# A graph layer on one core: two residual pieces go to GpSimd, tile 14's moments to ScalarE, and tile 14's result to the very end

## The reference

```python
h = jnp.maximum(_layernorm(x, axis=-1), 0.0)
x = x + _L0_gnn_ref(h, adj, ...)      # adj @ round(relu(q(h) @ q(weight))), 4-bit activations, 3-bit weights
h = jnp.maximum(_layernorm(x, axis=-1), 0.0)
x = x + _L1_gnn_ref(h, adj, ...)      # attention over the pairs with adj == 1
```

## Time and profile before

| what | value |
|---|---|
| median of 3 runs | 135.79 us (135.5 to 136.07) |
| profiled execution, its own time | 135.6 us |
| its span, first to last instruction | 133.8 us |
| PE, DVE, ACT, POOL busy | 88%, 84%, 72%, 56% of the span |
| share of PE on the chain that ended last | 72%, DVE 13% |
| granted TensorE clock, mean | 0.99 |

### The profile page before, as it was taken

How to read it: one execution, slowest core, us unless ns; L and a number is a source line. 1 busy time by engine, 2 the same in 40 slices (tenths; PEclk the granted TensorE clock), 3 DMA queues, 4 the chain that set the end, 5 groups by cost and what they waited for, 6 DMA issues and landing times.

```text
span 133.8 us, 2045 instructions
## 1 busy us (share of the span) xinstructions
PE 117.7 (88%) x597; PEld 71.5 (53%) x602; DVE 112.4 (84%) x255; ACT 96.1 (72%) x145; POOL 75.6 (56%) x105
## 2 busy tenths in 40 slices
PE   0198999999998799999999999999999999999600
PEld 0196445554553355554756656574756747647500
DVE  0689999969899867798969999999889999599880
ACT  3568787688779579757969999979992299862200
POOL 2463733354344843379935979884778978740120
PEclk9999999999999999999999999999999999999995
DMA  4999999954530999999395999218425265206422
GB/s 141 322 428 387 408 418 386 322 176 159 179 137 16 254 353 425 404 415 375 66 394 230 321 358 397 61 32 274 149 93 162 50 207 157 76 7 235 157 77 94
DMA packets 11712, 31.12 MB, mean 233 GB/s; under 512 B 1265, under 2 KB 4082, under 8 KB 10162
## 3 DMA queue, kind: packets, MB, share of 16 engines
q1 hardware_dynamic: 9010, 21.90, 43.9%
q10 hardware_dynamic: 1728, 6.69, 13.7%
q0 software_dynamic: 960, 2.36, 6.6%
HBM read 24.65 MB, written 6.29 MB: 231 GB/s over the span
## 4 chain that ended last, share of the span: by engine, by line
PE 72%; DVE 13%; issue 3%; ACT 2%; DVEq 0%; ACTq 0%
PE acc L1484 22%; PE acc L1471 21%; PE acc L1384 8%; PE acc L1402 8%; PE acc L1397 7%; DVE st L1025 3%; PE acc L1370 2%; PE acc L1452 2%; PE acc L1446 1%; DVE lo L1071 1%; ACT h_i L548 1%; DVE h_qT L1060 1%; DVE most L1077 1%; DVE sup L1065 1%; ACT z_sup L556 1%
## 5 line engine op out<-in xcount | busy, mean ns | idle before, releaser
L1484 PE MATMUL acc<-sup,lo 128*128 128x512 f32 x128 | 32.0, 402 | 0.0
L1471 PE MATMUL acc<-sup_h,hi 128*128 128x512 f16 x128 | 29.4, 380 | 0.0
L1484 PEld LDWEIGHTS acc<-sup,lo 128*128 128x128 f32 x128 | 24.1, 188 | 5.7
L1402 PE MATMUL acc<-sup,lo 128*128 128x512 f32 x64 | 25.0, 476 | 0.0
L531 ACT ACTIVATE junk<-raw,below 128x2048 uint8<-128x2048 f32 x12 | 23.9, 1993 | 0.4
L740 POOL TENSOR_TENSOR rs<-ve,minus_half 128x2 f32<-128x2 f32 (+2 forms) x16 | 14.6, 911 | 10.6 <-DVE ve L1035 10.3
L834 POOL DMA_INDIRECT raw<-adj_g,at_sb x12 | 16.6, 1381 | 6.4 <-DVE at_sb L1127 3.4
L752 POOL TENSOR_TENSOR lo<-raw,hi 128x512 fp32r<-128x512 f32 x11 | 13.0, 1197 | 12.4 <-DVE sup L1065 10.5
L523 ACT ACTIVATE hi<-raw 128x2048 f16<-128x2048 f32 x7 | 13.4, 1908 | 9.0 <-PE acc L1484 6.6
L1025 DVE BATCH_NORM_STATS2 st<-x_sb 128x6 f32<-128x512 f32 x29 | 19.5, 686 | 0.4
L1471 PEld LDWEIGHTS acc<-sup_h,hi 128*128 128x128 f16 x128 | 11.7, 98 | 15.1 <-issue 2.2
(11 more groups left out here) (126 smaller groups left out, 159.7 us busy)
## 6 DMA issues: line engine op xcount, KB each, us to landing
raw<-adj_t SPq DMA_DIRECT2D x10, 1024.0 KB, 10.6
raw<-adj_t ACTq DMA_DIRECT2D x8, 512.0 KB, 5.3
out<-ring SPq DMA_DIRECT2D x15, 256.0 KB
x_sb<-x SPq DMA_DIRECT2D x3, 1024.0 KB, 14.0
raw<-adj_t ACTq DMA_DIRECT2D x2, 1024.0 KB
sup_d<-sup_h SPq DMA_DIRECT2D x4, 512.0 KB
w_sb<-weight SPq DMA_DIRECT2D x4, 258.0 KB, 4.0
x_sb<-x SPq DMA_DIRECT2D x1, 512.0 KB, 5.7
```

The costliest lines, as they stand in the source:

```text
L1402: ins = nc.tensor.matmul(acc[t][:, :], part(lo, k % PARTS, at), sup[:, j, :], start=False, stop=(j == T - 1))
L1471: nc.tensor.matmul(bank[:, cols], part(hi, k % PARTS, j), sup_h[:, j, cols], start=(j == 0), stop=False)
L1484: ins = nc.tensor.matmul(bank[:, cols], part(lo, k % PARTS, j), sup[:, j, cols], start=False, stop=(j == T - 1))
```

## The change

There are three edits. GpSimd instead of VectorE makes `lo` of pieces 8 and 9 (`POOL_LO`, `PACED`). In the first stage `flag_half(n)` runs one step later for n from 1 on, so that the seventh and the eighth flag stand behind the last support tile, and `list_offsets` goes from step 9 to behind the eighth flag. In the tail, tile 14's mean and sum of squares come from two ACT passes with an accumulator (`moments`) in place of DVE's statistics, its variance and root are made by POOL behind tile 15's root, its result is DVE's last instruction, and it is stored in two column halves by ACT and SP.

```diff
-    POOL_LO = [0] + list(range(10, 4 * (GT + 1)))
-    PACED = {10: (8,), 12: (9, 10)} if POOL_LO[1] == 8 else {12: (10,)}
+    POOL_LO = [0] + list(range(8, 4 * (GT + 1)))
+    PACED = {10: (8,), 12: (9, 10)}
...
+        def store_part(eng, cols):
+
+            t = T - 2
+            eng.wait_ge(out_ready, t + 1)
+            eng.dma_start(out[t * P:(t + 1) * P, cols], ring[:, t % RING, cols]).then_inc(out_stored[t % RING], 16)
...
+            def moments(t):
+
+                act.wait_ge(x1_ready, t + 1)
+                act.wait_ge(out_stored[t % RING], 16 * (t // RING))
+                nc.scalar.activation(ring[:, t % RING, :], x_sb[:, t, :], ACT.Copy, scale=1.0 / D,
+                                     accum_out=mv[:, t, 0:1]).then_inc(x1_summed, 1)
+                act.wait_ge(x1_summed, 1)
+                nc.scalar.activation(ring[:, t % RING, :], x_sb[:, t, :], ACT.Square, bias=mv[:, t, 0:1], scale=-1.0,
+                                     accum_out=xs[:, 0, 1:2]).then_inc(x1_squared, 1)
+                act.wait_ge(x1_squared, 1)
+                nc.scalar.activation(ring[:, t % RING, :], x_sb[:, t, :], ACT.Relu, bias=mv[:, t, 0:1],
+                                     scale=-1.0).then_inc(yp_ready, 1)
...
             relu2(13)
-            relu2(14)
+            moments(T - 2)
             act.wait_ge(last_out_ready, 1)
             act.dma_start(out[(T - 1) * P:, halves[0]], ...)
+            store_part(act, halves[0])
...
-            for n in range(3, len(second_roots) - 1):
+            for n in range(3, len(second_roots) - 2):
                 second_root(n)
+            t = T - 2
             pool.wait_ge(last_var, 1)
             nc.gpsimd.tensor_tensor(rs[:, T - 1:T], mv[:, T - 1, 1:2], minus_half[:, 0:1], ALU.pow).then_inc(r_ready, 1)
+            pool.wait_ge(x1_squared, 1)
+            nc.gpsimd.tensor_scalar(ve[:, t:t + 1], xs[:, 0, 1:2], 1.0 / D, EPS, ALU.mult, ALU.add).then_inc(x1_var, 1)
+            pool.wait_ge(x1_var, 1)
+            inverse_root(t, 1)
...
             quantise_sup(8)
-            lo_of_piece(8)
             flag_half(0)
-            list_offsets()
             stats(14)
             bound_hT(10)
             quantise_sup(9)
-            lo_of_piece(9)
             normalise(first_no(15), stats(15))
-            flag_half(1)
             for j in range(11, T + 2):
                 if j < T:
                     bound_hT(j)
                 if j <= T:
                     quantise_sup(j - 1)
-                if j <= T - 1:
-                    flag_half(j - 9)
-                elif j == T:
+                if j <= T:
+                    flag_half(j - 10)
+                if j == T:
                     flag_half(7)
+                    list_offsets()
             list_values()
...
             result(13)
-            residual(14)
+            first_residual(T - 2)
             last_residual(T - 1)
-            result(14)
             dve.wait_ge(last_var, 1)
             last_result(T - 1)
+            result(T - 2)
```

More of the change, by code:

```diff
@@ L192, in gnn_kernel @@
         second_ln = [(0, 2), (2, 2)] + [(t, 1) for t in range(GT, T)]
-        second_roots = [(0, GT), (4, 4), (8, 2), (10, 2)] + [(t, 1) for t in range(12, T)]
+        second_roots = [(0, GT), (4, 4), (8, 2), (10, 2)] + [(12, 1), (13, 1), (15, 1), (14, 1)]
         FIRST = len(first_ln)
@@ L266, in gnn_kernel @@
         x1_ready = sem("x1_ready")
+        x1_summed = sem("x1_summed")
+        x1_squared = sem("x1_squared")
+        x1_var = sem("x1_var")
         yp_ready = sem("yp_ready")
@@ L469, in _ @@
                 load_adj(k)
-            for t in range(T - 1):
+            for t in range(T - 2):
                 store(t)
@@ L474, in _ @@
             store(T - 1)
+            store_part(sp, halves[1])
             for b in range(RING):
-                sp.wait_ge(out_stored[b], 16 * (T // RING + (b == (T - 1) % RING)))
+                sp.wait_ge(out_stored[b], 16 * (T // RING + (b >= (T - 2) % RING)))
             with sp.If(met > 0):
@@ L1147, in last_result @@
             def last_result(t):
-                n = FIRST + len(second_roots)
+                n = FIRST + root_no(t)
                 dve.wait_ge(out_stored[t % RING], 16 * (t // RING))
@@ L1287, in residual, with first_residual @@
                 variance(mean_var(step(ins), a, m), a, m)
+            def first_residual(t):
+                dve.wait_ge(acc_done, t + 1)
+                nc.vector.scalar_tensor_tensor(x_sb[:, t, :], acc[t % 8][:, :], cc(C_NEG), x_sb[:, t, :],
+                                               ALU.mult, ALU.subtract).then_inc(x1_ready, 1)
             def last_residual(t):
```

## The result

The changed kernel took 137.63 us (median of 4 runs, 137.32 to 138.21) where the kernel before took 135.84 beside it: ratio 1.0139, 95% interval 1.0095 to 1.0183. Measured again over 12 runs it was 137.14 against 135.67, ratio 1.0105 (1.0067 to 1.0142). It is slower, by 1.5 to 1.8 us; the prediction was 136.2 with a range to 137.1.

A forecast was written before the change was run, and what follows sets the result against it. PE bounds the kernel, through its idle time and the tail behind its last matmul. Front +0.5 and tail -0.1 gave +0.4 us, so 136.0 profiled and 136.2 as median, "no change"; range 134.9 to 137.1.

The forecast's parts named there:

- PE's two waits vanish: First stage, 40 to 46 us: PE no longer waits for DVE's h_qT and is 1.6 us early at 44 us.
- Chunk 4 lands at L = 54.7: ACT's load in the first stage: landing time L hardly moves from 54.93 us although issued 1.6 us earlier.
- Rival 1: Chunk 4 follows its issue, L = 53.3 to 53.9: -0.8 to -0.2 us in front, 134.9 to 135.5; chance 0.2.
- the sum of the queue rule: DMA engines take turns between queues, so chunk 4's landing follows its issue and the sum comes out 1.4 us lower.
- From S = L + 3.2, the list at L + 7.5: End of first stage: DVE's last support rows start at S, PE has the list at 62.2 us, against 61.66 before.
- rival 2: DVE's last offsets instruction is held by POOL, so the list misses one more piece: 1.1 us more, 137.3; chance 0.12.
- The argument against that hold: Against POOL holding DVE's small offsets row: DVE's ve rows of the same form ran beside POOL without being longer.
- Front +0.5: First stage: PE takes the list 0.5 us later than before, a shift that stays, with ends -0.8 and +0.8.
- DVE's last row ends 4.24 us behind PE's last: Tail: tile 14's result, now DVE's last instruction, ends nearest to 130.3 us against 130.22 before, +0.1 us.
- 2.2 to 2.8 us, and I take 2.6, -0.2.: End of the tail: landing time of the last stores, two 128 KB pieces of tile 14 leaving at once.
- Rival 3, the tail turns: POOL's scale and root for tile 14 both held behind tile 15's halves: tail +0.4 us, 136.7; chance 0.13.
- What would make it wrong: PE taking the list before 61.5 or after 62.8, or PE's end to span end differing from 7.7 us by over 0.6.

The follow-up runs named there:

- a_front: The changed first stage (new tables, flags and offsets) with the old tail, against the kernel before: ratio 1.005, 136.27 us.
- s_all_wait: Old first stage with the changed tail, but PE, DVE, ACT and POOL held before reading the flag until tiles 14 and 15's stores landed: ratio 1.0227, 138.74 us.
- t_before_wait: The kernel before, with all four engines held before reading the flag until the stores of tiles 14 and 15 landed: 138.19 us, one run.
- b_tail: The old first stage with the changed tail, against the kernel before: ratio 1.0062, 136.56 us.
- p_14_last: The kernel before, but SP issues tile 14's whole store behind its half of tile 15: ratio 1.0071.
- after: The first profiled execution of the whole changed kernel, which took 138.21 us; the kernel's median was 137.63 us.

## Why the prediction was wrong, step by step

- *PE's two waits vanish.* Right: supports at 40.37 and 43.27, forecast 40.55 and 43.45. The second wait was read 0.2 us too long, though: the row at 45.03 has 3 matmuls where the others have 4, and the next support follows it by 47.72 - 45.03 = 2.69 us and not 2.90, so the record of the support's first matmul is missing. The forecast support at 43.45 was thus 1.35 us early and not 1.6; measured, at 43.27, it was 1.5.
- *Chunk 4 lands at L = 54.7, nearer to "does not move".* The mechanism is right, the size a little low: 55.15 in the first profile, 54.60 in `a_front`. The issue moved by 0.98 us, not by 1.6. q1 alone moved at 47 to 48 us (46 packets, 99.8% of the engines), as in the earlier trace rows. Rival 1 (L = 53.3) fell, and with it the sum of the queue rule.
- *From S = L + 3.2, the list at L + 7.5.* Right: 58.27 is L + 3.12, and 62.58 is L + 7.43. The forecast for PE was 62.2. The instruction that was held was the offsets' last row and not the list, as rival 2 had it, but the list slipped through behind it: 0.21 us, not another piece. The argument against that hold had no row behind it: of the seven ve rows on 2 elements in the trace before, none lies inside a lo piece (the two that meet one begin 0.13 and 0.11 us ahead of its end). Front +0.5 forecast; 0.92 in the first profile, 0.6 us by `a_front`'s medians.
- *DVE's last row ends 4.24 us behind PE's last.* Right within 0.2: 4.08. POOL's scale was half held (0.48 us), its root began 0.56 us behind the scale's start.
- *"2.2 to 2.8 us, and I take 2.6, -0.2."* This step, the landing of the last stores, failed. The range was read from the one landing in the earlier trace rows, with the thought that two small pieces with little in front of them could only be quicker. Measured: 3.4 to 4.6. Two things stood in the sum at nothing: two stores leaving at the same moment, 0.45 us in `s_all_wait` against `t_before_wait`, and instruction packets on the DMA engines, which the queue tables of the kernel before have, 1.25 us in `s_all_wait` against `b_tail`. The tail came to +0.9 us (`b_tail`) where -0.1 was forecast, outside the -0.8 to +0.5 given.
- *Rival 3, the tail turns.* It had the sign and about half the size, by another mechanism (both held behind the halves), which occurred only in part (0.48 and 0.66 us for scale and root, against 0.19 and 0.54), and DVE ended no later for it. That half was luck.
- *What would make it wrong.* PE's last matmul to the end was to be 7.7 within 0.6; it was 136.5 - 126.97 = 9.5. The text's own test named the tail.

## What to carry to other kernels

PE's idle time that is removed ahead of a load is kept in full only if the load lands earlier too: look first at what stands in the queue ahead of it, and issue it in an idle stretch. In a tail, count the engines' hops behind the last matmul, not the work: moving two passes to an idle engine was worth 0.6%, and putting the other engine's root and the result behind everything else turned that into a loss of 0.6%. The landing of the last store is a term with its own spread, and the instruction packets that come while the engines end their parts belong in it.

## What the runs showed of the hardware

- An instruction packet of q8 (0.02 MB) keeps one DMA engine for 0.9 us (27.4% of 0.2 us x 16 in `p_14_last`) to 1.7 us (54.3% in `after`). Where it falls ahead of or into the last stores, 27 and 28 packets of theirs come singly after their bulk, over 1 and 2.1 us (`b_tail`, `after`). That these are the packets that wait for the same DMA engine fits but is not shown.
- Holding the four engines ahead of the flag took 1.05 and 1.25 us off the landing and put 3.8 us behind it. Which engine the packet belongs to, and whether the jump or just the progress of the code calls for it, stays open.
- A DVE operation on 4 elements (0.84 and 0.85 us) was held by a running POOL tensor_tensor like one on 64 (1.20 us), and the DVE operation queued directly behind it passed in 0.21 us. Each held row ended within 0.1 us of the end of a POOL piece.
- A load issued by one queue behind 1 MB of another's got nothing for some 3 us, as the earlier trace rows show, and an issue earlier by 0.73 us (`a_front`) and 0.98 us (`after`) moved the landing by -0.3 and +0.2 us.
